# Weights on another DMA queue, one store moved, and squared deviations summed on GpSimd before one averaging product

## The reference

```python
g = x.reshape(B, 32, 16, H, W)                      # 32 norm groups of 16 channels
m, s = mean(g, (2, 3, 4)), var(g, (2, 3, 4))        # one pair per image and group
n = (g - m) / sqrt(s + 1e-5)                        # normalised, back to (B, 512, H, W)

# quantised grouped 1x1 convolution on n: 4 groups of 128 channels, rotated by one
xa = round(clip((n - lA) / (uA - lA), 0, 1) * 15) / 15
wq = (round(clip((w - lW) / (uW - lW), 0, 1) * 15) / 15 - 0.5) * 2
y  = relu(einsum(xa, wq) * inv + (beta - running_mean * inv))
out = x + y + n                                     # two identities are added
```

## Time and profile before

| | |
|---|---|
| time, median of 3 runs | 258.81 us (258.80 to 259.05) |
| the profiled execution | 258.41 us |
| its span, first to last instruction | 256.7 us |
| mean granted TensorE clock | 0.902 of full speed |
| busy share over the span: VectorE, ScalarE, GpSimd, TensorE | 90%, 84%, 83%, 76% |
| HBM read and written | 51.65 MB and 51.38 MB |

### The profile page before, as it was taken

How to read it: one execution, slowest core, us unless ns; L and a number is a source line. 1 busy time by engine, 2 the same in 40 slices (tenths; PEclk the granted TensorE clock), 3 DMA queues, 4 the chain that set the end, 5 groups by cost and what they waited for, 6 DMA issues and landing times.

```text
span 256.7 us, 3463 instructions
## 1 busy us (share of the span) xinstructions
PE 193.9 (76%) x999; PEld 109.3 (43%) x999; DVE 230.0 (90%) x363; ACT 215.2 (84%) x394; POOL 212.0 (83%) x340
## 2 busy tenths in 40 slices
PE   1142996969889888979797997877696969889920
PEld 0132644435454444445443554343444435454510
DVE  2898698999999999999999899999999999969940
ACT  4437898999999999989999889999899888999300
POOL 6126869999999999999999999999999999999100
PEclk9999999797979798988979599999979797979995
DMA  6999999999999999999999999999999999999994
GB/s 225 398 411 411 408 409 406 418 416 417 418 414 418 417 416 418 411 418 416 416 415 416 418 416 413 419 417 415 417 413 418 416 418 409 402 400 402 393 399 193
DMA packets 34516, 103.25 MB, mean 402 GB/s; under 512 B 1202, under 2 KB 1730, under 8 KB 34498
## 3 DMA queue, kind: packets, MB, share of 16 engines
q1 hardware_dynamic: 18624, 54.86, 53.8%
q10 hardware_dynamic: 15874, 48.18, 47.0%
HBM read 51.65 MB, written 51.38 MB: 401 GB/s over the span
## 4 chain that ended last, share of the span: by engine, by line
POOL 52%; DVE 16%; issue 11%; PE 9%; ACT 5%; DMA 2%; DVEq 0%; SPq 0%; POOLq 0%; ACTq 0%
POOL images L413 27%; POOL levels L424 8%; DVE images L482 7%; PE prod L604 6%; DVE stats L460 4%; POOL dev L375 3%; DVE codes L475 3%; PE var_ps L584 3%; POOL dev L378 2%; DMA images<-in_x 2%; POOL scaled L404 2%; ACT levels L270 2%; POOL coef L406 2%; POOL norm L402 1%; ACT unused L242 1%
## 5 line engine op out<-in xcount | busy, mean ns | idle before, releaser
L604 PE MATMUL prod<-codes,w_t 128*128 128x392 bf16 x768 | 160.8, 369 | 7.9 <-DVE codes L475 2.9
L482 DVE SCALAR_TENSOR_TENSOR images<-prod,floor,images 128x784 f32<-128x784 f32 x128 | 128.0, 1019 | 8.5 <-PE prod L604 8.2
L413 POOL TENSOR_SCALAR images<-images,coef 128x784 f32<-128x784 f32 x120 | 123.7, 1042 | 0.0
L604 PEld LDWEIGHTS prod<-codes,w_t 128*128 128x128 bf16 x768 | 79.1, 110 | 81.6 <-issue 24.6
L270 ACT ACTIVATE levels<-images,coef 128x784 int16<-128x784 f32 x95 | 91.3, 1028 | 1.1 <-issue 1.1
L460 DVE BATCH_NORM_STATS2 stats<-images 128x6 f32<-128x392 f32 x136 | 68.9, 551 | 5.4 <-DMA images<-in_x 5.4
L236 ACT ACTIVATE unused<-images 128x784 bf16<-128x784 f32 x60 | 50.7, 847 | 7.5 <-DMA images<-in_x 5.2
L242 ACT ACTIVATE unused<-images,sums 128x784 bf16<-128x784 f32 x60 | 56.1, 939 | 0.1
L475 DVE TENSOR_SCALAR codes<-levels 128x3136 bf16<-128x3136 int16 x32 | 34.7, 1085 | 1.0 <-ACT levels L270 0.7
L584 PE MATMUL var_ps<-dev,avg 128*128 128x8 f32 x128 | 19.6, 280 | 20.0 <-POOL dev L382 20.0
L424 POOL TENSOR_SCALAR levels<-images,coef 128x784 int16<-128x784 f32 x33 | 33.6, 1020 | 0.1
(11 more groups left out here) (66 smaller groups left out, 83.2 us busy)
## 6 DMA issues: line engine op xcount, KB each, us to landing
images<-in_x SPq DMA_DIRECT2D x30, 1568.0 KB, 14.5
out<-images ACTq DMA_DIRECT2D x30, 1568.0 KB, 18.8
images<-in_x SPq DMA_DIRECT2D x8, 392.0 KB, 6.6
out<-images SPq DMA_DIRECT2D x1, 1568.0 KB, 8.8
out<-images SPq DMA_DIRECT2D x4, 392.0 KB, 7.4
w_raw<-in_weight SPq DMA_DIRECT2D x1, 256.0 KB, 6.5
rows<-in_channel_params ACTq DMA_DIRECT2D x1, 8.0 KB, 2.3
limit_row<-in_limits ACTq DMA_DIRECT2D x1, 0.0 KB
```

Of the source, the lines that this page charges most:

```text
L413: nc.gpsimd.tensor_scalar(here, here, coef[:, u % 2, 0, 1, G * j + o:G * j + o + 1], coef[:, u % 2, 1, 1, G * j + o:G * j + o + 1], ALU.mu ...
L482: nc.vector.scalar_tensor_tensor(out=two, in0=prod[:, k % SETS, :, 0:HALF], scalar=floor[:, o:o + 1], in1=two, op0=ALU.max, op1=ALU.add).t ...
L604: done = nc.tensor.matmul(prod[:, k % SETS, h, 0:HALF], w_t[:, part, output_group(g)], codes[:, n % 2, g, h * HALF:(h + 1) * HALF], start= ...
```

## The change

Three things are changed. The DMA of the weights is issued by ScalarE, third after the two small tables, and no longer by SyncE between image 0 and image 1. The store of image 0 is issued by SyncE, after the loads of images 2 to 11 and ahead of the load of image 12, which waits for that very store; ScalarE's first store is now that of image 1. In `deviations`, two more instructions of GpSimd add the four subsets of `dev2` pairwise, with a wait between them, and `average_deviations` becomes one product of eight columns.

```diff
-                if n == 0:
-                    sync.dma_start(w_raw[:], weight.rearrange("(g o) i -> o g i", o=P)).then_inc(weights_in, DMA)
...
-            for n in range(SINGLE, B):
+            for n in range(SINGLE, RING):
+                load(n)
+            store(0)
+            for n in range(RING, B):
                 load(n)
...
             act.dma_start(limit_row[:], limits).then_inc(limits_in, DMA)
+            act.dma_start(w_raw[:], weight.rearrange("(g o) i -> o g i", o=P)).then_inc(weights_in, DMA)
...
-                if 0 <= n < ACT_STORES:
+                if 0 < n < ACT_STORES:
...
+            FOLDS = 3
+
+            def folded(u, k, ins):
+                ins.then_inc(dev_step, 1)
+                pool.wait_ge(dev_step, FOLDS * u + k)
...
-                nc.gpsimd.tensor_tensor(dev[:, :, k:G], ...,
-                                        ALU.subtract).then_inc(dev_step, 1)
-                pool.wait_ge(dev_step, u + 1)
-                nc.gpsimd.tensor_tensor(dev2[:], dev[:], dev[:], ALU.mult).then_inc(dev_done, 1)
+                folded(u, 1, nc.gpsimd.tensor_tensor(dev[:, :, k:G], ..., ALU.subtract))
+                dev_ = dev[:].rearrange("p j g s -> p (j g) s")
+                folded(u, 2, nc.gpsimd.tensor_tensor(dev2[:], dev_, dev_, ALU.mult))
+                folded(u, 3, nc.gpsimd.tensor_tensor(dev2_half[:], dev2[:, :, 0:2], dev2[:, :, 2:4], ALU.add))
+                nc.gpsimd.tensor_tensor(dev2_sum[:], dev2_half[:, :, 0], dev2_half[:, :, 1], ALU.add).then_inc(dev_done, 1)
...
-                var = var_ps[:, 0:2 * G].rearrange("p (j g) -> p j g", g=G)
-                for s in range(SUBSETS):
-                    done = nc.tensor.matmul(var, avg[:], dev2[:, :, :, s], start=False, stop=(s == SUBSETS - 1))
-                done.then_inc(var_done, 1)
+                nc.tensor.matmul(var_ps[:, 0:2 * G], avg[:], dev2_sum[:], start=False, stop=True).then_inc(var_done, 1)
```

More of the change, by code:

```diff
@@ L100, in fused_norm_quantised_conv @@
         dev = sb("dev", [P, 2, G, SUBSETS], F32)
-        dev2 = sb("dev2", [P, 2, G, SUBSETS], F32)
+        dev2 = sb("dev2", [P, 2 * G, SUBSETS], F32)
+        dev2_half = sb("dev2_half", [P, 2 * G, SUBSETS // 2], F32)
+        dev2_sum = sb("dev2_sum", [P, 2 * G], F32)
         half_var = sb("half_var", [P, 2 * G], F32)
@@ L377, in deviations @@
                 own = sums[:, par, 0].unsqueeze(3)
-                nc.gpsimd.tensor_tensor(dev[:, :, k:G], own[:, :, k:G].to_broadcast([P, 2, G - k, SUBSETS]),
-                                        mean[:, :, k:G].to_broadcast([P, 2, G - k, SUBSETS]),
-                                        ALU.subtract).then_inc(dev_step, 1)
-                pool.wait_ge(dev_step, u + 1)
-                nc.gpsimd.tensor_tensor(dev2[:], dev[:], dev[:], ALU.mult).then_inc(dev_done, 1)
+                folded(u, 1, nc.gpsimd.tensor_tensor(dev[:, :, k:G], own[:, :, k:G].to_broadcast([P, 2, G - k, SUBSETS]),
+                                                     mean[:, :, k:G].to_broadcast([P, 2, G - k, SUBSETS]), ALU.subtract))
+                dev_ = dev[:].rearrange("p j g s -> p (j g) s")
+                folded(u, 2, nc.gpsimd.tensor_tensor(dev2[:], dev_, dev_, ALU.mult))
+                folded(u, 3, nc.gpsimd.tensor_tensor(dev2_half[:], dev2[:, :, 0:2], dev2[:, :, 2:4], ALU.add))
+                nc.gpsimd.tensor_tensor(dev2_sum[:], dev2_half[:, :, 0], dev2_half[:, :, 1], ALU.add).then_inc(dev_done, 1)
             LINKS = 6
```

## The result

| | before | after |
|---|---|---|
| time, median of 5 runs | 258.81 us | 262.33 us |
| range of the runs | 258.66 to 259.19 | 262.01 to 263.65 |
| ratio (95% interval) | | 1.0141 (1.0121 to 1.0161) |
| span of the profiled execution | 256.7 us | 260.3 us |
| last `finish` of VectorE ends | 246.93 us | 253.90 us |

A forecast was written before the change was run, and what follows sets the result against it. GpSimd paces, compute and the memory stream ending nearly together. Compute 8.0 - 1.3 - 0.7 - 0.7 = 5.3 us later, less 1.6 at the end, adds 3.7: 262.5 us, case range 259.5 to 265, overall 258.6 to 265.2.

The forecast's parts named there:

- The two adds: GpSimd, pairs 2 to 15: 0.57 us more in each of 14 blocks, 8.0 us later in all.
- the slow pair: The pair at 146.66 to 161.24 us, 1.37 us longer than others: its excess may go, -0.7 us.
- The start: Pairs 0 and 1: shorter TensorE products gain up to 1.6 us, less 0.3 for the weights, so 1.3 us.
- The weights. They come earlier, but VectorE is not kept waiting by them: Start: the moved weights' DMA does not delay VectorE; 0.3 us taken off for competing with image 0's load.
- The end's product: Last pair's product on TensorE, on the chain with VectorE waiting behind it: 0.7 us less.
- Sum of compute: Whole kernel: compute ends 5.3 us later, from 8.0 - 1.3 - 0.7 - 0.7.
- The end gives back 1.6: After image 30's store is issued: 11.2 us to the last bytes in place of 12.8, giving back 1.6.
- On a dry stream the least is 8.0 plus the fixed part of a DMA, 3.1 - 0.95 = 2.1: End: at least 10.1 us from issue of image 30's store to the last bytes.
- The store of image 0, 0 ± 0.4: Store moved to SyncE: changes the order of bytes, not their number; 0, between -0.4 and +0.4 us.
- that TensorE and VectorE pace: Rival: the loop from TensorE to VectorE paces, GpSimd only looks full; faster, at best 257.9 us, chance 0.08.
- That the stream absorbs it: Rival: compute ends at most 2 us later and the DMA stream hides it; 258.8 us, chance 0.10.
- The clock: Rival: TensorE, less busy, runs at its lower clock level in more pairs; 266 us, chance 0.08.

The follow-up runs named there:

- e5: Kernel before plus the two adds on GpSimd, their result unused, four products kept, queues as before: ratio 1.0216.
- e6: Kernel before with one product over subset 0 and no adds, three of four subsets left out of the variance: ratio 0.9984.
- e3: Changed kernel with weights and store of image 0 put back, leaving only the two adds and single product: ratio 1.0036 against before.
- e2: Kernel before with only the store of image 0 moved to SyncE: ratio 1.0039.
- e11: Changed kernel with the weights back on SyncE, so adds, single product and moved store of image 0: ratio 1.0029 against before.
- e4: Changed kernel with the weights as ScalarE's first DMA, ahead of the two small tables: ratio 1.0072 against before.
- e10: Changed kernel with the store of image 0 back on ScalarE, so adds, single product and moved weights: ratio 1.0093 against before.
- e1: Kernel before with only the weights' DMA moved to ScalarE's queue: ratio 1.0010.
- e9: Kernel before with the store of image 0 kept on ScalarE but issued with that of image 1: ratio 1.0018.

## Why the prediction came out right

The pace was read rightly: GpSimd sets it, and the adds lengthen each pair. That the time came out right to 0.2 us is luck all the same: compute ended 1.7 us later than forecast, and the end gave back 1.8 us more.

- **The two adds, 8.0 us, and the slow pair, -0.7: together 7.3 forecast, 8.1 measured.** From `coef` of pair 1 to that of pair 14 the change added 7.5 us, in the last pair 0.6. The mechanism was right: 0.58 at the place itself, and e5 and e6 show the cause. The slow pair did vanish, but not by what the prediction says of it alone: it is the pair with three stalls of `cap`, and with its counterpart of one stall (13.21) it stood 0.7 above two of the usual 13.93. The usual pair itself grew by 0.62, from 13.93 to 14.55, where 0.57 was worked out. In all traces the pairs of three stalls come right behind a stretch of over 6 us with the clock granted at 0.50, which is the part of the prediction's account that holds; but such a stretch does not suffice, for the changed kernel has one from 102 to 108 us (columns as above), and no pair of three:

```profile
102.00:108.00 6.00, 5.61 (x18) 2.82 (x19) 5.07 (x10) 5.09 (x14) 5.45 (x13) 0.50 1.03 416
```

- **The start, -1.3.** Mis-sized, it was -0.18. Adds and product gave more than the 1.6 that I let through (2.4 in e3), and the step that failed is "The weights. They come earlier, but VectorE is not kept waiting by them": they came 2 us later (11.1 in place of 9.14, issue 2.64 and 6.5 to landing), and cost 2.1 to 3.3 us where I had taken 0.3. I priced 256 KB by the stream's mean rate, and not by the queue in front of them.
- **The end's product, -0.7:** after the last `coef`, 7.96 us late, the last finish was 6.97 late, so 1.0.
- **Sum of compute:** 5.3 forecast, 6.97 measured.
- **The end gives back 1.6.** Mis-sized, it was 3.4: from 9.8 us to 6.4 after the last finish. The step that failed is "On a dry stream the least is 8.0 plus the fixed part of a DMA, 3.1 - 0.95 = 2.1". Between the issue of the store of image 30 (250.16) and the stream's stop (259.0) there are 8.8 us, less than that floor. The 2.1 are all that a DMA takes from issue to landing beside its bytes; what the stream loses is only the part before the first bytes, about 0.9 us here (250.16 to 251.1) and as much in e3 (247.33 to 248.2), and behind it come 7.9 us for 3.21 MB at 405 GB/s. And the fade of four microseconds went away altogether.
- **The store of image 0, 0 ± 0.4.** Not confirmed: alone it costs 1.0 (e2), with the folds nothing (e11).

The rivals: that TensorE and VectorE pace fell by e5 and e6. That the stream absorbs it is true of each part apart (0 to 3.4 us are hidden) and false of the whole. The clock: after ran at 0.885 against 0.902, but of the 13 pairs none was longer than 14.72 us, so the period shows no cost of it. By span, every run that ends dry lies 6.4 us after its last finish (e3, e4, e10, e11, after; e5 6.9), and those whose last finish is before 250.3, which is 256.7 - 6.4, lie at 256.3 to 258.0. Added up, the parts alone give 0.3 + 1.0 + 0.9 = 2.2 us, the whole 3.5; the difference is mostly the weights' delay, which e1 could hide. What stays open is how much the store adds to the whole. After against e10, which lacks it, is 262.3 to 261.7 us, and 1.0141 (from 1.0121) to 1.0093 (to 1.0116) as ratios, so 0.6 to 1.2 us; but e11 against e3 shows nothing. The profiled execution of e10 was its slowest (262.53), so its span of 260.8 is no measure for this. And two ranges stand in the prediction, 259.5 to 265 and 258.6 to 265.2; the measured time lies in both.

## What to carry to other kernels

When a memory stream and an engine end nearly together, find the point from which a delay is seen (here 3.4 us of compute), and sum the delays of all parts of a change before comparing them with it: alone, only the folds exceeded it, by 0.7. An engine with no waits at all pays for each instruction put on it, however short, and each linked one near its pitch from start to start (about 0.25 us by the periods, 0.28 in the earlier trace rows), while the engine that is relieved may have had nothing to give. What a DMA costs can depend on what is queued before it more than on its bytes: issued first on ScalarE and not third, one microsecond earlier, the weights landed 6 us sooner.

## What the runs showed that was not expected

- The stream that is full until the end fades: 532 KB over 252 to 256 us. Run a little dry, it keeps 405 GB/s to its last microsecond. So 3 us of late compute were nearly free: 0.3 us by e1.
- Stores alone moved 401 GB/s (53 to 57 us of e9), mixed with loads 417 (50 to 60 us of before). A load that went out 4.7 us late cost 0.5 us by that alone (0.2 to 0.7).
- While GpSimd is never idle, each `cap` of VectorE stalls it once, wherever it falls, and a pair is short or long by how many fall into it: 13.21, 13.9 and 15.34 us for one, two and three before.
- The weights (256 KB) landed 6.1 to 7.1 us after issue on SyncE's queue behind four tiles, 9.3 to 10.5 as ScalarE's third DMA, and 4.0 and 4.1 as its first.
